# Block attention with a mixture of experts: reordered logits and seam, units of one tile, VectorE combining two late tiles

## The reference

```
q, k, v = xn Wq' + bq, xn Wk' + bk, xn Wv' + bv
theta   = 0.5 + 0.2 sigmoid(qk) + 0.15 tanh(qk) + 0.1 relu(qk)      qk = q k', 1024 x 1024 for each of 4 batches
s       = softmax(theta) v Wo' + bo
expert  = argmax(xn Wr + br)                                        8 experts, one for each token
g       = silu(gelu(xn W1[e] + b1[e]) W2[e] + b2[e])                256 -> 1024 -> 256, float32
out     = x + s * g
```

## Time and profile before

| | |
|---|---|
| median of 3 runs | 536.84 us (536.63 to 537.06) |
| the profiled execution's own time | 537.1 us |
| its span | 535.4 us |
| PE busy | 517.5 us (97%) |
| DVE, ACT, POOL busy | 408.2, 335.2, 195.4 us |
| granted clock of PE | full over the whole span but its last slice |

### The profile page before, as it was taken

How to read it: one execution, slowest core, us unless ns; L and a number is a source line. 1 busy time by engine, 2 the same in 40 slices (tenths; PEclk the granted TensorE clock), 3 DMA queues, 4 the chain that set the end, 5 groups by cost and what they waited for, 6 DMA issues and landing times.

```text
span 535.4 us, 10760 instructions
## 1 busy us (share of the span) xinstructions
PE 517.5 (97%) x3779; PEld 484.8 (91%) x3779; DVE 408.2 (76%) x810; ACT 335.2 (63%) x611; POOL 195.4 (36%) x230
## 2 busy tenths in 40 slices
PE   7998999999999999999999979999999999999996
PEld 6888899899989999899999969988899988999996
DVE  6897688955758855498555688758999999777896
ACT  3488778535536634266334464678777887877882
POOL 2226337931222212322112222004577685343443
PEclk9999999999999999999999999999999999999999
DMA  8942920027314731145311421005123232211121
GB/s 279 352 160 99 353 81 1 1 51 245 118 60 131 233 111 39 60 131 206 138 39 39 130 72 40 22 21 184 56 97 106 73 118 90 61 48 41 60 61 59
DMA packets 40323, 57.09 MB, mean 107 GB/s; under 512 B 3607, under 2 KB 35358, under 8 KB 39726
## 3 DMA queue, kind: packets, MB, share of 16 engines
q1 hardware_dynamic: 35020, 45.62, 25.5%
q0 software_dynamic: 3488, 9.47, 6.1%
q10 hardware_dynamic: 1762, 1.32, 0.8%
HBM read 40.68 MB, written 17.56 MB: 109 GB/s over the span
## 4 chain that ended last, share of the span: by engine, by line
PE 83%; DVE 8%; ACT 5%; issue 2%; DMA 2%; ACTq 0%; POOL 0%; POOLq 0%; DVEq 0%
PE ps L855 25%; PE ps L857 24%; PE ps L856 24%; PE ps L954 5%; DVE stats L1316 1%; PE ps L1137 1%; PE ps L1021 1%; DMA row<-xn_rows,unit_token 1%; ACT hid L731 1%; PE ps L1011 1%; DVE theta L1374 1%; DVE theta L1370 1%; DMA xn_all<-in_L_attn_x_dram 1%; ACT theta L618 1%; ACT theta L608 1%
## 5 line engine op out<-in xcount | busy, mean ns | idle before, releaser
L855 PE MATMUL ps<-v_hi,pT_hi 128*128 128x258 f32 x256 | 76.4, 298 | 2.2 <-issue 0.8
L856 PE MATMUL ps<-v_lo,pT_hi 128*128 128x258 f32 x256 | 72.4, 283 | 0.0
L717 ACT ACTIVATE hid<-ps,b_now 128x256 f32<-128x256 f32 x128 | 53.6, 471 | 30.0 <-PE ps L857 29.1
L857 PE MATMUL ps<-v_hi,pT_lo 128*128 128x258 f32 x256 | 72.2, 282 | 0.0
L1370 DVE SCALAR_TENSOR_TENSOR theta<-tanh_s,theta 128x512 f32<-128x512 f32 x64 | 48.8, 763 | 20.7 <-ACT tanh_s L609 20.0
L618 ACT ACTIVATE theta<-theta,neg_max 128x512 f32<-128x512 f32 x64 | 42.9, 721 | 29.9 <-DVE neg_max L1374 29.8
L855 PE MATMUL ps<-w_hi_even,hidT_h 128*128 128x256 f32 x200 | 58.1, 290 | 3.2 <-DVE hidT_l L1658 3.2
L739 ACT ACTIVATE g_sb<-y_sb 128x512 f32<-128x512 f32 x20 | 12.6, 632 | 71.7 <-DVE y_sb L1663 71.7
L499 POOL COPY unit_token<-sorted_token 128x2 int32 x19 | 3.7, 195 | 147.1 <-PE ps L1137 147.1
L857 PE MATMUL ps<-w_hi_even,hidT_l 128*128 128x256 f32 x200 | 56.6, 283 | 0.0
L856 PE MATMUL ps<-w_lo_even,hidT_h 128*128 128x256 f32 x200 | 56.6, 283 | 0.0
(11 more groups left out here) (248 smaller groups left out, 1648.6 us busy)
## 6 DMA issues: line engine op xcount, KB each, us to landing
w_raw_odd<-in_L_ffn_W_dram SPq DMA_DIRECT2D x10, 1024.0 KB, 5.7
w_raw_even<-in_L_ffn_W_dram SPq DMA_DIRECT2D x6, 1024.0 KB, 6.5
sorted_g<-g_sb SPq DMA_DIRECT2D x20, 256.0 KB, 2.2
xn_rows<-xn_all SPq DMA_DIRECT2D x4, 1024.0 KB, 6.1
x_tile<-in_L_attn_x_dram SPq DMA_DIRECT2D x32, 128.0 KB, 2.2
out_dram<-g_tile SPq DMA_DIRECT2D x32, 128.0 KB, 1.7
xn_all<-in_L_attn_x_dram SPq DMA_DIRECT2D x3, 1024.0 KB, 12.4
kept_xT<-passing_xT SPq DMA_DIRECT2D x2, 1024.0 KB, 4.1
```

The lines of the kernel that those rows point to most:

```text
L717: last = nc.scalar.activation(hid[:, j % 2, c * UNIT:(c + 1) * UNIT], ps[:, HID_BANK + j, c * UNIT:(c + 1) * UNIT], ACT.Gelu, bias=b1_now[ ...
L855: mm(dst, a_hi, b_hi, start=first, stop=False)
L856: mm(dst, a_hi, b_lo, start=False, stop=False)
L857: return mm(dst, a_lo, b_hi, start=False, stop=last)
```

## The change

- **Logits.** The constant products for `attn_const` move behind G's products; ACT and DVE make `G_hi` and `G_lo` ahead of the second half of acts(0) and of the first half of thetas(0). `take_turned(0)` moves ahead of the third `low_v`. Transposes of xn go in pairs of `turn` calls, ACT keeps q = 3 ahead of q = 2, and values(0) and values(1) wait for three copies instead of four.
- **Small products in groups.** `route` and `invert` calls go in groups of four blocks instead of one or two behind each block.
- **Lone units.** Gelu, parts and products go in four steps of two chunks; for the last two steps ACT makes the high part too. Where the lone unit is an expert's first, ACT and DVE do the first half of the next W1 beside it, ahead of the gelus. PE's wait for W1 moves from above the branch into the first product that needs it.
- **Seam.** exps(8) goes with acts(8), with the table of exp loaded there and the one of gelu loaded again ahead of the last unit; acts(9) runs before exp's table comes back; DVE does thetas(9) ahead of `biased(last_u)`.
- **End.** ACT makes both halves of `pT_hi` of tiles 9, 30 and 31 too. thetas(31) goes whole ahead of tile 30's parts; PE splits values(30) around transposes(31), which goes to other banks; DVE combines tiles 29 and 30; POOL's last tile, 28, waits for thetas(31).

```diff
-    ROUTING = (3, 4, 5, TPB)
+    ROUTING = (3, 4, 5, TPB, TPB + 1, NT - 2, NT - 1)
...
+        def pT_bank(n, h):
+
+            return ps[:, (S_BANK if n == NT - 1 else PT_BANK) + h, :]
...
-        HALF_STEPS = [None, (0, 2), (2, 4), (4, 8)]
...
+        KEPT_ORDER = [(0, 1), (3, 2)]
...
+            for p, n in enumerate(COMBINED[:LATE]):
                 spot, turn = p % RING, p // RING + 1
...
+                for q in [p + AHEAD] if p + 1 < LATE else range(p + AHEAD, NT):
+                    if q >= RING:
+                        pool.wait_ge(out_sent[q % RING], 16 * (q // RING))
+                    gather(q)
+                if p + 1 == LATE:
+                    pool.wait_ge(theta_done, NT)
...
                 if n in ROUTING:
                     act.wait_ge(pT_done, n * 2 + 1)
-                    nc.scalar.activation(pT_hi[n % 2][:, 0:TPB // 2, :], blocks_of(ps[:, PT_BANK, :]), ACT.Copy
+                    nc.scalar.activation(pT_hi[n % 2][:, 0:TPB // 2, :], blocks_of(pT_bank(n, 0)), ACT.Copy
                                          ).then_inc(pT_hi0, 1)
                 act.wait_ge(pT_done, n * 2 + 2)
-                nc.scalar.activation(pT_hi[n % 2][:, TPB // 2:, :], blocks_of(ps[:, PT_BANK + 1, :]), ACT.Copy
+                nc.scalar.activation(pT_hi[n % 2][:, TPB // 2:, :], blocks_of(pT_bank(n, 1)), ACT.Copy
                                      ).then_inc(pT_hi1, 1)
...
             act.wait_ge(c_ready, 1)
-            for h in range(2):
-                acts(0, h)
+            acts(0, 0)
             act.wait_ge(G_done, 1)
             nc.scalar.activation(G_hi[:, :, :], pair_of(ps[:, 7, :]), ACT.Copy).then_inc(G_high, 1)
+            acts(0, 1)
             for q in range(2):
                 keep_turned(0, q)
             exps(0)
@@ -681,7 +693,7 @@
...
                         if n < 3:
-                            for q in range(2 * h, 2 * h + 2):
+                            for q in KEPT_ORDER[h]:
                                 keep_turned(n, q)
...
                 act.wait_ge(hidT_ready, u * 4 + 1)
-                nc.scalar.activation(hid[:, 0, :], ps[:, HID_BANK, :], ACT.Copy).then_inc(gelu_done, 1)
-                for s in range(1, 4):
-                    first, stop = HALF_STEPS[s]
-                    act.wait_ge(hid_done, u * 4 + 3 + stop // 8)
-                    for c in range(first, stop):
+                nc.scalar.activation(hid[:, 0, :], ps[:, HID_BANK, :], ACT.Copy).then_inc(act_kept, 1)
+                if beside:
+                    beside()
+                for s in range(4):
+                    act.wait_ge(hid_done, u * 4 + 3 + s // 2)
+                    for c in range(2 * s, 2 * s + 2):
                         last = nc.scalar.activation(
-                            half_gelus(s)[:, c - first, :], ps[:, HID_BANK + 2 + c // 4, c % 4 * P:(c % 4 + 1) * P],
+                            half_gelus(s)[:, c % 2, :], ps[:, HID_BANK + 2 + c // 4, c % 4 * P:(c % 4 + 1) * P],
                             ACT.Gelu, bias=b1_now[:, par, c:c + 1])
-                    last.then_inc(gelu_done, 1)
+                    if s < 2:
+                        last.then_inc(gelu_done, 1)
+                last.then_inc(act_kept, 1)
+                wait_apart(act, act_kept, u * 2 + 2)
+                for s in range(2, 4):
+                    nc.scalar.activation(hidT_h[:, 2 * s:2 * s + 2, 0:P], half_gelus(s), ACT.Copy).then_inc(gelu_done, 1)
...
                 with act.If(u0 < full):
                     gelus(u0, par)
+                    row_high(u0 + 1)
+                    high_w1(w1_landed, other, raw[0], slice(0, 1))
                 with act.If(full < u0 + 1):
-                    gelus_half(u0, par)
-                row_high(u0 + 1)
-                raw = raw_of(e + 1)
-                high_w1((w1_in[place_of(e + 1)], landed(e + 1)), other, raw[0], both)
+                    gelus_half(u0, par, beside=lambda: high_w1(w1_landed, other, raw[0], slice(0, 1)))
+                    row_high(u0 + 1)
+                high_w1(w1_landed, other, raw[0], slice(1, 2))
...
                     acts(TPB, h)
+                nc.scalar.activation(warm[:, 2:3], zeros[:, 0:1], ACT.Exp)
+                exps(TPB)
...
+            nc.scalar.activation(warm[:, 3:4], zeros[:, 0:1], ACT.Gelu)
             with act.If(last_u < full_7):
                 gelus(last_u, 1)
             with act.If(full_7 < last_u + 1):
                 gelus_half(last_u, 1)


-            nc.scalar.activation(warm[:, 3:4], zeros[:, 0:1], ACT.Exp)
-            exps(TPB)
             for h in range(2):
                 acts(TPB + 1, h)
+            nc.scalar.activation(warm[:, 3:4], zeros[:, 0:1], ACT.Exp)
...
@@ -931,8 +955,9 @@
                                        G_hi[:, k, :], G_lo[:, k, :], k == 0, k == DC - 1)
                     if i == 1:
                         last.then_inc(v_done, 1)
-                    if routed_batch is not None:
-                        route(routed_batch, 2 * q + i)
+                if routed_batch is not None and q % 2:
+                    for t in range(2 * q - 2, 2 * q + 2):
+                        route(routed_batch, t)
...
+                        if turned_batch is not None and k == 0:
+                            turn(turned_batch, 2 * h)
+                            turn(turned_batch, 2 * h + 1)
...
-                            ps[:, PT_BANK + h, i * P:(i + 1) * P],
+                            pT_bank(n, h)[:, i * P:(i + 1) * P],
...
                 at = place_of_batch(n // TPB)
-                for i in range(TPB):
-                    if n < NT - 1 and i % 4 == 0:
+                for i in blocks:
+                    if i % 4 == 0:
                         pe.wait_ge(pT_ready, n * 2 + i // 4 + 1)
-                    elif n == NT - 1 and i in (0, 2, 4):
-                        pe.wait_ge(pT_ready, n * 2 + i // 2 + 1)
...
-                    if routed_batch is not None:
-                        route(routed_batch, i)
+                    if routed_batch is not None and i % 4 == 3:
+                        for t in range(i - 3, i + 1):
+                            route(routed_batch, t)
                     for t in inverted[i] if inverted else ():
...
-            for ec in range(DC):
-                mm(ps[:, PT_BANK, 0:D], bv_wide[:, ec, :], woT[:, ec, :], start=ec == 0, stop=False)
-            mm(ps[:, PT_BANK, 0:D], ones[0:1, :], bo_row[:, :], start=False, stop=True).then_inc(const_done, 1)
...
                         last.then_inc(G_done, 1)
                     route_0(4 + 2 * m + ec)
+            for ec in range(DC):
+                mm(ps[:, PT_BANK, 0:D], bv_wide[:, ec, :], woT[:, ec, :], start=ec == 0, stop=False)
+            mm(ps[:, PT_BANK, 0:D], ones[0:1, :], bo_row[:, :], start=False, stop=True).then_inc(const_done, 1)
...
-                    pe.wait_ge(turned_kept, 4 * n + 4)
+                    pe.wait_ge(turned_kept, 4 * n + 3)
...
-            values(n - 2, inverted=[[i] for i in range(TPB)], limited="ends")
-            values(n - 1, inverted=[[TPB + 2 * i, TPB + 2 * i + 1] for i in range(TPB)], limited="full")
+            values(n - 2, inverted=[range(i - 3, i + 1) if i % 4 == 3 else () for i in range(TPB)], limited="ends")
+            values(n - 1, inverted=[range(TPB + 2 * i - 2, TPB + 2 * i + 2) if i % 2 else () for i in range(TPB)], limited="full")
...
-                    if c == HC // 2:
-                        pe.wait_ge(w1_split, split)
+                    if c % (HC // 2) == 0:
+                        pe.wait_ge(w1_split, split - 1 + c // (HC // 2))
...
-                    if h:
-                        pe.wait_ge(w1_split, split)
+                    pe.wait_ge(w1_split, split - 1 + h)
...
                     if h == 0:
-                        pe.wait_ge(gelu_done, u * 4 + 1)
+                        pe.wait_ge(act_kept, u * 2 + 1)
                     else:
                         if following:
                             turn_rows(u + 1)
-                        pe.wait_ge(hidT_ready, u * 4 + 3)
+                        pe.wait_ge(dve_kept, u + 1)
...
-                for s in range(1, 4):
-                    pe.wait_ge(hidT_ready, u * 4 + s + 3)
-                    for c in range(*HALF_STEPS[s]):
-                        last = tile_out(0, par, c)
+                for c in range(HC):
+                    if c % 2 == 0:
+                        pe.wait_ge(hidT_ready, u * 4 + c // 2 + 3)
+                    last = tile_out(0, par, c)
...
-                pe.wait_ge(w1_split, split - 1)
                 with pe.If(u0 < full):
...
-            weighted(NT - 2)
+
+            pe.wait_ge(half_s_ready, NT - 3)
+            values(NT - 2, blocks=range(0, TPB // 2))
+            pe.wait_ge(acts_done, (NT - 1) * 2)
             transposes(NT - 1)
+            values(NT - 2, blocks=range(TPB // 2, TPB))
             weighted(NT - 1)
...
-            thetas(0, [0])
             dve.wait_ge(G_high, 1)
```

(59 more changed lines are left out.)

## The result

The changed kernel takes 533.65 us (median of 20 runs, 533.05 to 536.52), the kernel before 537.03 in runs beside it. The ratio is 0.9944, 95% interval 0.9933 to 0.9954: 3.0 us faster, 2.5 to 3.6 (the two medians are 3.4 apart). Forecast were 531.1 us and a gain of 5.7. The range held the time (529.4 to 533.9), but at its upper end; four to five tenths of the gain are missing. The profiled execution has a span of 531.9 us, 3.5 less than before's.

A forecast was written before the change was run, and what follows sets the result against it. PE's work plus its gaps was taken as the bound, with the work kept. Logits -1.4, lone units -1.8, seam -1.4, end -1.1 and groups 0 sum to -5.7: 531.1 us against the median, range 529.4 to 533.9.

The forecast's parts named there:

- Lone units: Four lone units: shorter PE waits and an earlier branch, -1.8 us in sum, bounds -0.8 and -2.3.
- the term -0.9: Expert whose first unit is lone: branching ahead gives -1.2, a wait of about 0.3 remains, net -0.9 us.
- Rival 3: Experts' openings: exposed branches at 1.08 us each make it slower, 539.7 us with seven and the last; chance 0.04.
- Small products in groups, 0: `route` and `invert` groups: entering a group has one price at either length, so 0 gain, bounds -0.6 and +0.4.
- rival 2: Small products: switches cost 0.08 each, so groups save some 1.5 us more, giving 529.5 us; chance 0.09.
- Logits, -1.4: Early batches' logits and values: reordering shortens PE's waits, -1.4 us in sum, bounds -2.2 and -0.4.
- (a): Logits of batch 0: the `G_lo` wait goes, but PE waits 1.0 for `c_half`; net +0.4 instead of -0.6.
- (b): Logits: the wait for the next batch's `c_half` shrinks, 0.3 remaining one batch later; -1.0 us.
- Lone units behind full ones, -0.9: Two lone units behind full units: the second PE wait shortens by 0.45 each, -0.9 for both.
- Seam, -1.4: Tiles 8 and 9: the first wait goes, 0.3 of the second remains; -1.4 us, bounds 0 and -1.8.
- End, -1.1: Last tiles: both waits before transposes(31) and its parts go, a 0.3 wait comes; -1.1 us, bounds -0.3 and -1.5.

The follow-up runs named there:

- e8: The kernel before, with only the last expert's loop code placed in the second half of a 256-instruction block; 536.82 us, ratio 0.9999.
- e1: The changed kernel with the last expert's loop code placed in the second half of a 256-instruction block; 531.58 us, ratio 0.9907.
- e9: e5 with the router's small products one or two behind each block again, inverts still in groups; 530.34 us, ratio 0.9883.
- e13: e5 with the 16 reads of loop limits moved beside `u_product(1, q)` and `v_product(1, q)`; 529.71 us, ratio 0.9871.
- e14: e13 with the inverts one or two behind each block as before; 529.59 us, ratio 0.9866.
- e11: e1 with the order of the logits as in the kernel before, groups of small products kept; 532.40 us, ratio 0.9925.
- e5: e1 with batch 0's four transposes groups each behind its own product instead of in pairs; 530.61 us, ratio 0.9886.
- e6: e1 with the seam as in the kernel before; 532.83 us, ratio 0.9927.
- e7: e1 with the end as in the kernel before; 532.61 us, ratio 0.9918.
- base 1: The changed kernel with the edit of e1, used as base for further runs; 531.58 us.
- e4: The changed kernel with the inverts one or two behind each block again instead of in groups of four; 535.65 us, ratio 0.9974.
- e2: The changed kernel with PE's wait for W1's first half back above the branch of every expert and the last one; 535.05 us, ratio 0.9965.
- e3: The changed kernel with the first half of the next W1 made after the lone first unit again, not beside it; 534.72 us, ratio 0.9968.
- e15: The changed kernel with the last loop's code at place 32 of the same 256-instruction block instead of 0; 535.01 us, ratio 0.9966.
- e10: e5 with the first pair of `turn` calls of batches 2 and 1 behind the second product; 530.23 us, ratio 0.9882.
- e12: e5 with DVE's `low_w1` between the second and third step of the lone first unit; 530.32 us, ratio 0.9883.
- e16: e5 with the edits of e10 and e13 together; 529.56 us, ratio 0.9867.

## Why the prediction was right in kind and wrong in size

**The step that failed** is in "Lone units", of the expert whose first unit is the lone one: "PE then branches ahead, because the last parts are there 1.3 us before PE is through with them, more than the 1.08 of the branch. That gives -1.2", and with it the term -0.9. The mechanism was right in each part: the first wait grew by 0.7, the second went, PE left the unit 3.0 earlier, the branch came ahead of the end of PE's queue by 1.1 us. The price of the branch was wrong. The 1.08 of the earlier trace rows was not the price of a branch: 0.59 of it was W1 (e8), and the rest was the tail of a fetch that had been running beside the wait for W1. When the fetch begins only at the branch, the branch takes 3.75 us, and 2.59 of idle time show. The term came out at +1.15 in place of -0.9, and in 7 executions of 20 the clock added 1.7. With the code in place (e1) the second rows of the last expert come at 335.32 against 339.42, 4.10 ahead, where the lead of that run was 2.88 at the rows behind the second lone unit (301.48 against 304.36): -1.2, a little better than the -0.9.

Rival 3 had named the mechanism, with the price of 1.08 for each of six openings or more; it came at one opening, with 2.59 us idle instead of 1.08.

**Small products in groups, 0.** Of the groups themselves this was right (e9: 0; e13 and e14: 0.1 or less), and rival 2 falls. Its price didn't follow from its own counts either: 0.08 for each of 24 + 12 + 14 is 4.0 us and not 1.5, and the groups of inverts fell from 16 to 6, by 10 and not 14. The stretch with the inverts still gained 0.86, below the bound of -0.6. The prediction said that the reads "pace PE's instruction stream and stay where they are"; what it missed is that a stretch paced by reads moves when its first read does.

**Logits, -1.4.** Measured -0.8 (e11: 0.8). (a) came as forecast and a little worse, transposes(0) 0.58 later for +0.4; the wait of 1.0 was foreseen and by e5 it was needless. Residues of the waits for `c_half` were 0.67 and 0.61 instead of 0.3 and took most of the rest. The first of them stood in the rows: 1.3 less the 0.69 of the third `low_v` leaves 0.6, but (b) took 0.3 from the batch behind.

**Lone units behind full ones, -0.9.** Measured -0.96 on the timelines, over the whole stretch from transposes(7); no run takes this part back.

**Seam, -1.4.** By the lead at its two sides 0.8; by taking it back (e6) 1.25 in time, 1.5 in the trace. The first wait went, the second left 0.27 idle where 0.3 was forecast. What is missing is a third wait that the forecast didn't price, for `u_lo`, before the first product behind transposes(10). PE in the kernel before, then ACT in the changed one:

```profile
369.21 0.48 PE L855 MATMUL ps<-xnT_hi,M_hi 128*128 128x512 f32 x1
```

```profile
365.47 0.67 ACT L581 ACTIVATE u_hi<-ps,r_col 128x512 fp32r<-128x512 f32 x1
```

From the transposes to that product it was 0.84 us (368.37 to 369.21) and is 1.53 (365.45 to 366.98), 0.69 more. ACT makes `u_hi` behind exps of the next tile. In the kernel before it started at 367.66, so it is 2.2 earlier, while PE's transposes are 2.9 earlier. ACT's chain gained just the 0.75 that the forecast gave it (acts(10) at 361.05 instead of 361.8); PE can't gain more than its chain at the next thing it needs from it. The 1.25 of e6 is larger because the lone units' two high parts, which the forecast had charged to the seam (0.8), stay there.

**End, -1.1.** The trace gives -1.1, e7 1.03. DVE's combining fits, with 0.47 idle left before the last steps. The minimum of tile 31's first half took 0.69 us at 518.36, where it took 1.12 beside POOL: POOL's work had been moved from under it. What ran beside it was not the multiply of the earlier trace rows, which ended at 520.35, but the add behind it:

```profile
520.43 1.07 POOL L526 TENSOR_TENSOR g_tile<-g_tile,x_tile 128x256 f32<-128x256 f32 x1
```

The rule of the Trainium skill (SBUF — State Buffer, "Who interferes with whom") is borne out in kind: the minimum took 0.43 longer beside POOL's add, of which 0.57 was left when it started, and not the whole 1.07.

The sum of the measured terms: -0.78 - 0.86 - 0.96 + 1.15 - 0.76 - 1.21 = -3.42. With -1.2 for the lone first unit it is -5.8, and base 1 measured 5.3 less than before by the medians, 5.9 by the two profiled executions. That this is so near the forecast of -5.7 is in part luck: logits and seam came out 1.2 short together, and the 0.86 of the inverts, which the forecast had at 0, filled most of that. Of the 2.3 us that the changed kernel lacks, 2.05 are the one branch.

## What to carry to other kernels

Before a wait is taken away from above a branch, look at the branch's record and at where its target's code lies: behind a wait a branch can look cheap (0.66 us here) because its code was coming meanwhile, and cost 3.7 us where nothing hides the fetch; moving the loop to another half of a block gave 2.1 us (1.8 against the executions without a fall of the clock). Where an in-order sequencer reads registers between products, those reads are the chain, and most of what is put ahead of the first read is lost (0.8 of 1.0 us in e4). When a wait is taken away, follow the late engine's chain to the next thing that PE needs from it, since the gain ends there (`u_lo` at the seam). And what taking a part back measures depends on which other parts stay in: the seam is 0.8 by one way and 1.25 by the other.

## What was not expected of the hardware

- The branch into the last expert's loop took 3.27 to 3.89 us in five kernels (the changed one, e2, e3, e4, e15), and 0.29 where the loop lay in the other half of a block (e1). In these five and in the kernel before it ended 1.5 us behind the end of a 16 KB packet of instructions.
- The granted clock fell to half for 3.4 us behind a PE gap of 2.3 to 2.7 us in 7 of 20, 6 of 6, 7 of 7, 7 of 8 and 6 of 7 executions (the changed kernel, e2, e3, e4, e15), and behind one of 1.2 in 2 of 5 (e11). It did not fall in the 42 executions of e1, e5 to e7, e9, e10, e12 to e14 and e16, though all but e12 keep a gap of 1.3 before the lone first unit's first product and e6 has one more. Nor did it in the kernel before, which has a gap of 1.14 at the place of e11's. Length alone doesn't decide; what else does is open.
- A read of a register from SBUF holds PE's stream for 0.65 us (0.30 of it the load itself), 16 of them for some 10 us; taking them out of that stretch saved 0.9 us of the whole.
